# A two-layer network on one core: new places in the instruction order, column groups for two products, keys sent by GpSimd

## The reference, cut to what matters

```python
x = LN(x + attention(x))            # 16 heads of 16 dims, one shared key and value head
x = LN(x + ffn(x))                  # 256 -> 1024, exact GELU, ternary weights, 1024 -> 256
x = LN(x + L1_attn(x))              # see below
x = LN(x + mx_linear(x))            # 256 -> 256, blocks of 32 rounded to an fp6 grid
```

## Time and profile before

| what | value |
|---|---|
| median of 3 runs | 1768.9 us |
| the profiled execution's own time | 1771.4 us |
| its span | 1769.6 us |
| TensorE matmul busy | 1637.5 us (93%) |
| VectorE / ScalarE / GpSimd busy | 1343.4 / 1293.2 / 1104.3 us |
| mean granted TensorE clock | 0.966 of full speed |
| instructions in the span | 84556 |

### The profile page before, as it was taken

How to read it: one execution, slowest core, us unless ns; L and a number is a source line. 1 busy time by engine, 2 the same in 40 slices (tenths; PEclk the granted TensorE clock), 3 DMA queues, 4 the chain that set the end, 5 groups by cost and what they waited for, 6 DMA issues and landing times.

```text
span 1769.6 us, 84556 instructions
## 1 busy us (share of the span) xinstructions
PE 1637.5 (93%) x35371; PEld 1189.0 (67%) x35371; DVE 1343.4 (76%) x2605; ACT 1293.2 (73%) x2601; POOL 1104.3 (62%) x3392
## 2 busy tenths in 40 slices
PE   5768999999999999999999999999999999999865
PEld 4535667677777777677777777777777767776643
DVE  5546778888788888888888888888888888887454
ACT  3437777788787888778887778887788877887521
POOL 5002346767677776676777767777677776767732
PEclk8879999999999999999999999999999999999875
DMA  9963334444244433444333444334443344431010
GB/s 239 203 93 54 60 58 62 74 72 69 51 72 73 73 66 58 67 73 72 70 61 62 74 72 69 61 62 74 71 71 61 62 71 71 73 58 32 18 29 20
DMA packets 133765, 125.18 MB, mean 71 GB/s; under 512 B 18965, under 2 KB 130633, under 8 KB 133385
## 3 DMA queue, kind: packets, MB, share of 16 engines
q1 hardware_dynamic: 129184, 119.50, 39.1%
q10 hardware_dynamic: 4200, 0.27, 0.2%
HBM read 33.73 MB, written 18.87 MB: 30 GB/s over the span
## 4 chain that ended last, share of the span: by engine, by line
PE 53%; POOL 15%; ACT 10%; issue 8%; DVE 4%; DMA 4%; SPq 4%; POOLq 0%; DVEq 0%; ACTq 0%
PE value_bank L772 11%; PE gen_bank L910 8%; PE score_banks L750 7%; PE gen_bank L598 6%; PE max_banks L590 6%; PE gate_bank L803 5%; ACT L1130 4%; ACT probs L1130 3%; PE gen_bank L819 3%; PE gate_bank L598 2%; POOL square L1613 2%; POOL rstd L1598 2%; DMA key_pieces<-khalf 2%; POOL diff L1717 2%; POOL hseq L1722 2%
## 5 line engine op out<-in xcount | busy, mean ns | idle before, releaser
L1186 DVE TENSOR_REDUCE nmax<-max_banks 128x2 f32<-128x1024 f32 x512 | 622.5, 1216 | 65.3 <-PE max_banks L592 61.3
L1130 ACT ACTIVATE probs<-score_banks 128x1024 f32<-128x1024 f32 x512 | 525.0, 1025 | 112.3 <-PE score_banks L752 96.3
L772 PE MATMUL value_bank<-probs,vaug 128*32 128x128 f32 x8192 | 327.3, 278 | 1.1 <-issue 1.1
L772 PEld LDWEIGHTS value_bank<-probs,vaug 128*32 128x32 f32 x8192 | 205.5, 110 | 90.6 <-issue 79.7
L590 PE MATMUL max_banks<-kaug,qaug 62*128 62x512 f32 x512 | 238.7, 466 | 24.8 <-DVE nmax L1186 15.7
L750 PE MATMUL score_banks<-qaug,kaug 64*128 64x512 f32 x512 | 237.6, 464 | 12.4 <-ACT probs L1130 7.8
L1717 POOL TENSOR_TENSOR diff<-gates 128x16 f32<-128x16 f32 x472 | 114.2, 242 | 212.3 <-ACT gates L1135 205.1
L592 PE MATMUL max_banks<-kaug,qaug 62*128 62x512 f32 x512 | 239.2, 467 | 0.4 <-issue 0.4
L752 PE MATMUL score_banks<-qaug,kaug 64*128 64x512 f32 x512 | 237.6, 464 | 0.0
L1135 ACT ACTIVATE gates<-gate_bank 128x48 f32<-128x48 f32 x472 | 99.0, 210 | 167.6 <-PE gate_bank L803 167.2
L803 PEld LDWEIGHTS gate_bank<-hseq,ghT 128*32 128x32 f32 x11328 | 159.1, 112 | 81.3 <-POOL hseq L1722 57.4
(11 more groups left out here) (234 smaller groups left out, 3540.6 us busy)
## 6 DMA issues: line engine op xcount, KB each, us to landing
qstage<-qhalf SPq DMA_DIRECT2D x384, 128.0 KB
qstage<-qhalf SPq DMA_DIRECT2D x128, 112.0 KB
xt<-in_L_attn_x SPq DMA_DIRECT2D x64, 128.0 KB
xk<-in_L_attn_x SPq DMA_DIRECT2D x16, 512.0 KB, 8.7
residual<-x2s SPq DMA_DIRECT2D x64, 128.0 KB
x2f<-residual SPq DMA_DIRECT2D x64, 128.0 KB
out<-x SPq DMA_DIRECT2D x64, 128.0 KB
qaug<-nmT SPq DMA_DIRECT2D x256, 8.0 KB, 1.8
```

The lines of the kernel that those rows point to most:

```text
L772: last = pe.matmul(value_bank[32 * g:32 * g + 32, :].rearrange("p (k t) -> p k t", k=HG)[:, :, u * BLOCK_POS:(u + 1) * BLOCK_POS], vaug[:, ...
L1130: act.activation(probs[:, beat % 2, :, :], score_banks[:, :, :], ACT.Exp).then_inc(exp_done, 1)
L1186: dve.tensor_reduce(nmax[:, m % 2, at:at + 9:8], max_banks[:, :, :], AX_X, ALU.max, negate=True).then_inc(max_taken, 1)
```

## The change

All places are chosen anew. `OWN_AT` gives turns -2 to 5 places of their own, and `place` and `beat_at` look there first; `LAST_AT`, for turn 64, is empty. INPUT stands at -2, which is place 254 of the turn before. HLOA now stands at 260, one turn later. A list `QUARTERED` names what TensorE does in column groups: the same as before, and now also FFN1A, FFN1B and ATT. A transpose in column groups is a matmul with the identity (`turned_block`). `store_keys` and `place_keys` are begun by GpSimd in its set-up instead of by SP.

The diff, cut to its core. Of the eight own turns, three stand here in part; in the others each table is of the same kind.

```diff
-PE_AT = dict(INPUT=0, F2_0=275, F2_1=280, F2_2=285, F2_3=285, F2_4=286, F2_5=288, F2_6=299, F2_7=302, TURND=279, LAST=322, XT=50, Q=12, OUT=128, OT=65, ATT=73, PROJ=90, TURNX=149, B=160, X1T=217, NM=204, FFN1A=247, FFN1B=249)
-ACT_AT = dict(OT=44, TURND=339, XT=104, Q=29, Q8=253, TURNX=196, ATT=145, X1T=230, GELUA=238, GELUB=239, X1=194, X2=178, X4=496)
-DVE_AT = dict(Q=23, X4R=362, X2R=52, OT=62, X3R=171, X3=239, QUANT=240, XN=148, LN1=157, BS=190, SCAN=236, ORDER=182, X1P=216, HLOA=240, NM=216)
-POOL_AT = dict(LN4=418, LN3=97, LN2=6, LNI=8, QIN=192, X2S=77, XD=214, X3B=193, LN1=15, X1B=116, STATES=165, HLOB=219)
-SP_AT = dict(MOVE=15, X2F=200, STORE=89, OUTST=406, XLD=59, NMPLACE=95)
+PE_AT = dict(INPUT=-2, F2_0=274, F2_1=275, F2_2=278, F2_3=278, F2_4=296, F2_5=297, F2_6=299, F2_7=304, TURND=309, LAST=336, XT=63, Q=8, OUT=134, OT=69, ATT=87, PROJ=100, TURNX=173, B=213, X1T=221, NM=217, FFN1A=240, FFN1B=247)
+ACT_AT = dict(OT=43, TURND=307, XT=51, Q=41, Q8=239, TURNX=158, ATT=99, X1T=193, GELUA=224, GELUB=236, X1=151, X2=202, X4=455)
+DVE_AT = dict(Q=27, X4R=371, X2R=85, OT=97, X3R=189, X3=205, QUANT=252, XN=141, LN1=145, BS=215, SCAN=238, ORDER=203, X1P=234, HLOA=260, NM=220)
+POOL_AT = dict(LN4=384, LN3=101, LN2=45, LNI=61, QIN=201, X2S=204, XD=222, X3B=200, LN1=96, X1B=217, STATES=154, HLOB=204)
+SP_AT = dict(MOVE=34, X2F=66, STORE=108, OUTST=365, XLD=46, NMPLACE=71)
 BEAT_AT = dict(
-    SCORES=(19, 61, 89, 107, 137, 157, 178, 231),
-    PAIR=(18, 55, 87, 102, 140, 202, 236, 250),
-    VALUES=(11, 68, 100, 128, 151, 157, 224, 252),
-    STEP=(15, 51, 72, 93, 135, 156, 166, 229),
-    EXP=(86, 121, 165, 181, 186, 227, 228, 236),
-    TANH=(46, 90, 125, 170, 181, 196, 227, 235),
-    MAX=(17, 26, 60, 107, 160, 190, 213, 233),
-    MIX=(3, 4, 12, 13, 20, 34, 96, 157),
+    SCORES=(14, 61, 99, 113, 154, 185, 216, 230),
+    PAIR=(14, 62, 97, 128, 168, 217, 230, 254),
+    VALUES=(3, 87, 111, 130, 180, 203, 227, 240),
+    STEP=(10, 74, 94, 112, 143, 209, 223, 240),
+    EXP=(49, 97, 121, 132, 142, 168, 179, 210),
+    TANH=(34, 66, 101, 128, 137, 174, 198, 224),
+    MAX=(15, 42, 96, 129, 165, 203, 216, 245),
+    MIX=(3, 61, 72, 80, 97, 109, 132, 133),
 )
+OWN_AT = {
...
+    -1: dict(
+        PE=dict(NM=142),
+        DVE=dict(NM=183),
+        SP=dict(NMPLACE=190),
+        BEAT=dict(PAIR=(-1, -1, -1, -1, -1, 36, 197, 211), MAX=(-1, -1, -1, -1, -1, -1, 12, 221)),
+    ),
+    0: dict(
+        PE=dict(XT=1, Q=0, NM=170),
+        ACT=dict(XT=144, Q=28),
+        DVE=dict(Q=11, ORDER=142, NM=142),
+        SP=dict(MOVE=90, XLD=91, NMPLACE=90),
+        BEAT=dict(SCORES=(34, 35, 88, 127, 150, 172, 175, 220), PAIR=(21, 35, 74, 136, 161, 172, 211, 226), VALUES=(-1, 50, 119, 138, 143, 183, 189, 215), EXP=(33, 39, 98, 101, 159, 230, 236, 250), MAX=(10, 14, 89, 102, 133, 141, 209, 243)),
+    ),
...
+    2: dict(
+        PE=dict(F2_0=35, F2_1=35, F2_2=43, F2_3=46, F2_4=47, F2_5=51, F2_6=52, F2_7=56, XT=73, Q=23, OT=81, ATT=94, PROJ=116, TURNX=127, B=151, X1T=182, NM=204, FFN1A=237, FFN1B=240),
+        ACT=dict(OT=10, XT=122, Q=10, TURNX=129, ATT=100, X1T=144, GELUA=187, GELUB=249, X1=133, X2=123),
...
+}
+LAST_AT = dict(
+)
+QUARTERED = ("INPUT", "LAST", "Q", "OUT", "ATT", "PROJ", "B", "FFN1A", "FFN1B")
...
-    def tile_at(table, name, kind, n, at):
-
-        late, slot = divmod(table[name], SLOTS)
+    tables = dict(PE=PE_AT, ACT=ACT_AT, DVE=DVE_AT, POOL=POOL_AT, SP=SP_AT)
+
+    def own(n):
+
+        return LAST_AT if n == TILES else OWN_AT.get(n, {})
+
+    def place(engine, name, n):
+
+        return own(n).get(engine, {}).get(name, tables[engine][name] % SLOTS)
+
+    def tile_at(engine, name, kind, n, at):
+
+        late = tables[engine][name] // SLOTS
         m = n - late + LEAD[kind]
-        return m if at == slot and live(m) and (kind not in ("X", "Q", "LOAD") or n - late >= 0) else None
-
-    def beat_at(name, at):
-
-        return BEAT_AT[name].index(at) if at in BEAT_AT[name] else None
+        return m if at == place(engine, name, n) and live(m) and (kind not in ("X", "Q", "LOAD") or n - late >= 0) else None
+
+    def beat_at(name, n, at):
+
+        slots = own(n).get("BEAT", {}).get(name, BEAT_AT[name])
+        return slots.index(at) if at in slots else None
...
-                slot = PE_AT[name] + SLOTS * (m - LEAD[kind])
+                n = m - LEAD[kind] + PE_AT[name] // SLOTS
+                slot = SLOTS * n + place("PE", name, n)
...
-            def in_quarters(out, weights, moving, start, stop):
-
+            def multiplied(name, out, weights, moving, start, stop):
+
+                if name not in QUARTERED:
+                    return pe.matmul(out(slice(0, P)), weights, moving, start=start, stop=stop, skip_group_check=True)
                 for q in range(0, P, 32):
-                    last = pe.matmul(out(q), weights[:, q:q + 32], moving, start=start, stop=stop, tile_position=(0, q), skip_group_check=True)
+                    last = pe.matmul(out(slice(q, q + 32)), weights[:, q:q + 32], moving, start=start, stop=stop,
+                                     tile_position=(0, q), skip_group_check=True)
                 return last
+
+            def turned_block(name, out, src):
+
+                if name not in QUARTERED:
+                    return pe.transpose(out(slice(0, P)), src, ident[:, :])
+                return multiplied(name, out, src, ident[:, :], True, True)
...
-                    turn_tile(g0, att).then_inc(filled[0], 1)
+                    turn_tile("ATT", g0, att).then_inc(filled[0], 1)
...
-                                    last = pe.matmul(gen_bank[half][:, f * P:(f + 1) * P], w1Tb[:, k, (4 * half + f) * P:(4 * half + f + 1) * P],
-                                                     x1piece[:, piece, k, :], start=(piece + f + k == 0), stop=(piece == 2 and k == KT - 1),
-                                                     skip_group_check=True)
+                                    last = multiplied(("FFN1A", "FFN1B")[half], lambda rows: gen_bank[half][rows, f * P:(f + 1) * P],
+                                                   w1Tb[:, k, (4 * half + f) * P:(4 * half + f + 1) * P], x1piece[:, piece, k, :],
+                                                   piece + f + k == 0, piece == 2 and k == KT - 1)
...
+            def store_keys(r):
+
+                pool.wait_ge(k_split, r + 1)
+                settle(pool)
+                pool.dma_start(k_dram[r].rearrange("t c f -> (t c) f"), khalf[:, :, :].bitcast(F32).rearrange("p a s -> p (a s)")).then_inc(k_written, 16)
+
+            def place_keys(r):
+
+                pool.wait_ge(k_written, 16 * (r + 1))
+                pool.wait_ge(ones_set, 2 * r + 3)
+                settle(pool)
+                for at, g, piece in PLACES:
+                    dims = min(DK, SPLIT - g * DK)
+                    pool.dma_start(kaug[at + g * DK:at + g * DK + dims, r, :, :, :].bitcast(F32).rearrange("d t u s -> d t (u s)"),
+                                 k_dram[r, :, 0:dims, piece * S:(piece + 1) * S].rearrange("t d f -> d t f")).then_inc(k_placed[r], 16)
+
+            for r in range(2):
+                store_keys(r)
+                place_keys(r)
+            store_keys(2)
...
             assert link[0] == BIASES_SPLIT
+            place_keys(2)
+            store_keys(3)
...
+            place_keys(3)
```

More of the change, by code:

```diff
@@ L608, in turn_x @@
                 for k in range(KT):
-                    last = pe.transpose(gen_bank[1][:, k * P:(k + 1) * P], xt[:, m % XR, k * P:(k + 1) * P], ident[:, :])
+                    last = turned_block("XT", lambda rows: gen_bank[1][rows, k * P:(k + 1) * P], xt[:, m % XR, k * P:(k + 1) * P])
                 last.then_inc(filled[1], 1)
@@ L617, in make_queries @@
                     for k in range(KT):
-                        last = in_quarters(lambda q: gen_bank[1][q:q + 32, o * P:(o + 1) * P], wqT[:, k, o * P:(o + 1) * P], xTq[:, k, :],
-                                           k == 0, k == KT - 1)
+                        last = multiplied("Q", lambda rows: gen_bank[1][rows, o * P:(o + 1) * P], wqT[:, k, o * P:(o + 1) * P], xTq[:, k, :],
+                                       k == 0, k == KT - 1)
                 last.then_inc(filled[1], 1)
@@ L781, in input_bias @@
                 wait(pe, tanh_done, STEPS * (m - (bank is not gate_bank)))
-                in_quarters(lambda q: bank[q:q + 32, 0:STEPS * GW], bias_rows, gate_of[:, :, :, :].rearrange("a k g b -> a (k g b)"), True, False)
+                multiplied("INPUT", lambda rows: bank[rows, 0:STEPS * GW], bias_rows[:, :], gate_of[:, :, :, :].rearrange("a k g b -> a (k g b)"), True, False)
             def input_gate(m, bank, g):
                 gate = bank[:, 0:STEPS * GW].rearrange("p (k g b) -> p g k b", k=STEPS, g=3)
-                in_quarters(lambda q: gate[q:q + 32, g, :, :], gcT[:, g, :],
-                            states[:, m // R % 2:m // R % 2 + 1, m % R * STEPS:(m % R + 1) * STEPS, :].rearrange("p a s b -> p (a s) b"),
```

(19 more changed lines are left out.)

97 lines of the change are left out of this document (58 added, 39 removed).

## The result

The changed kernel takes 1906.44 us (median of 4 runs, 1900.80 to 1909.45) beside 1771.12 for the one before on the same chip: a ratio of 1.0761, interval 1.0728 to 1.0794. The forecast was 1812, at most 1865. The direction and the place were right, the size was not: 135 us more instead of 43.

What follows compares the result with a forecast made beforehand. TensorE, busy 93% of the span, was taken as the bound, with the order within a tile and its instruction stream deciding. 1771.4 + 66 - 8 - 16 + 1 = 1814.4 us profiled, less 2.5: 1812 us; range 1745 to 1865.

Steps and rivals of the forecast that it cites:

- The instructions: First layer in column groups: blocks used up before the next comes, stalls 1.8 us a tile, net 1.05, +66 us.
- rival of 1746 us: Instruction fetch keeps up, a block of 1.8 us in the first layer passes without a stop: faster, chance 0.20.
- The order: New places within a tile: +0.5 around the scores, -0.65 later, so -0.15 us a tile, -8 us.
- The queries' wait: Queries' matmul needs the bank the second GELU empties: TensorE waits 0.65 us a tile, which hides stalls.
- The stream: First layer's bf16 column groups take 54 to 56 ns for 128 columns, as whole matmuls do: no gain.
- rival of 109 ns: First layer's groups stream at the f32 group's 109 ns: +160 us, 1972 us, chance 0.01.
- The start: Set-up and first tiles: keys' transfers off SP -3, tile 2's queries sooner -6, own places -7; together -16 us.
- the keys' own waits: Set-up, keys' transfers begun by GpSimd: from a gain of 8 to a loss of 5, taken as -3 us.
- the queries of tile 2: Start: freed from behind the keys in SP's queue, their transfers start 3.5 us sooner: -6 us (-1 to -11).
- +66: Block stalls from column groups, net 1.05 us a tile over 63 tiles, in us; range 0 to +205.
- The end: Last turn makes tile 59's input part for nobody and again for the tail: +1 us (0 to 1.6).
- dearer: Rival: order costs 0.5 to 1 us a tile more, or blocks nearer 4 us: 1840 to 1870, chance 0.20.

Runs made afterwards that it cites:

- small transfers: From tile 9 on, the queries' 8 transfers cut to 4 rows of 1 KB each: 1855 us in the changed kernel, 1769 us with the first layer whole.

## Why the forecast missed, step by step

**The instructions: right in kind, too small.** 359 blocks, stops on borders in runs of 128x32 bf16 matmuls, none when the groups go. I took 3.1 us as the least time between borders; the stops show 3.6. With it the stops in and behind the first layer are 2.10 us a tile, not 1.8: +16 us. (The quickest block that passed without a stop in the kernel before took 4.11 us, not 4.18; nothing hangs on it.) The Trainium skill (Runtime: NRT & Kernel Launch, Instruction fetch mechanics) calls the crossing of such a border "mostly hidden"; here it is for nearly all blocks that last 4 us or more while the DMA engines are idle, and isn't where they last 2.5. Its 2048 instructions for TensorE, which gave my rival of 1746 us, are not borne out: a stretch of 384 dense ones stops already, and no block began less than 1.16 us after the end of its fetch.

**The stops under the queries' transfers: missing.** This step of the forecast failed outright. I had written that the stops of before "fell where the DMA engines had work (share 0.41 between two of them)", and used that only to take the lower figure for the first layer, where the share is 0.08. What the new order puts beside the transfers 5 to 9 us into a tile I didn't count: 0.90 us a tile instead of 0.15, about +40 us.

**The order.** Forecast -0.15 us a tile, measured +0.26 (24.59 without stops against 24.33): +22 us. From the last scores to the next tile's second it gained 0.3 us, not 0.4; the later stretch lost 0.56, not 0.29. A wait that I hadn't found is the turn of the maxima (0.2 to 0.5 us more behind the pair before it). A larger one that the forecast doesn't price is that of the next tile's second scores for the exponentials. TensorE's waits in tiles 9 to 61 of the changed kernel, us in total, times, longest:

```profile
PE score_banks L807 <- ACT probs L1190: 26.1, 53, 0.6
```

The kernel before waited so for 1.4 us in 6 waits, and with x4 behind the GELUs and the first layer whole it is still 28.5 us in 53. How much of the period it costs isn't shown, since no run takes it away. The queries' wait was nearly right, 0.55 in the typical row and 0.45 on the mean for 0.65, and so was its being hidden: the fitted period without stops is 24.07 in the changed kernel and 24.69 with the first layer whole.

**The stream** at 54 ns a bf16 group: right, and the rival of 109 ns is excluded. The Trainium skill (TensorEngine Tiling (Array Packing), Restrictions) has column tiling give up the fast weight load; 2.63 against 2.63 us show no price for it here. fp32 turns, by contrast, went from 0.37 to 0.44, the +0.07 of the forecast.

**The start.** Own places gained 8 to 10 us (7 forecast), but in tiles 0 and 1: the ramp tiles 2 to 8, which were to give the 7, take 160.3 us instead of 161.4 with own places alone. The keys on GpSimd cost 9 to 12 us at tile 9, where the forecast had a gain of 9: 3 for the keys' own waits (a loss of 5 as the worst) and 6 for the queries of tile 2. I had bounded the issues' own time and not what they do to the transfers beside them. SP didn't begin the queries of tile 2 sooner (at 100.45 us, 99.33 before), and they were cast at 120.06 (113.69 before) instead of before 110. Tile 9 starts 8 us later; the forecast had 16 earlier, with some 7 us of its +66 falling into the tiles ahead of tile 9. That is +17 us. **The end** took 3 us less, not 1 more.

1812 + 16 + 40 + 22 + 17 - 4 = 1903, and some 7 for the part of the stops that was not hidden (0.62 us a tile instead of 0.75): 1910 for the 1906 measured. The fitted periods are good to about 0.1 us a tile, 5 us in this sum (the two runs with the first layer whole and the same places give 24.58 and 24.69). The range failed because stops, order and start all missed to the same side: I had given "dearer" one mechanism more, not three.

## What to carry to other kernels

Splitting an operation multiplies TensorE's instructions, and they come in blocks: count, for every point of the loop, how long 256 matmuls and loads last, and keep it above 3.6 us where the DMA engines are idle and near 5.4 us where they are full. These are values of this kernel, not sharp limits: under full engines a stretch of 5.4 us stopped for 0.15 us a tile and one of 4.2 for 0.7 to 0.9, single blocks of 4.0 us passed, and some of up to 7.3 were stopped for. Take the split where it shortens the stream (fp32, 1.05 us a tile) and leave it where it doesn't (bf16). And test an order with the stops taken out: one place on ScalarE was worth some 40 us and could not be seen while TensorE stood at block borders.

## What the runs showed that I had not expected

- Between the start of a fetch and TensorE's going on lie 2.3 to 2.6 us with idle DMA engines and 3.1 to 3.4 with full ones; a fetch takes 0.95 to 1.1 us in the one case and 1.75 in the other, and the fetches of blocks that were stopped for start up to 5.7 us after their border. Single fetches start as late with small transfers too, and what delays those isn't shown.
- 64-column groups cost nothing that can be told (ratio 1.0230 beside 1.0262 whole) where 32-column groups cost 90 us: the price doesn't go by the number of instructions.
- Eight transfers issued by GpSimd took 4.2 to 4.4 us, and SyncE's next eight 8.6 and 8.3 us in two kernels with the keys there, against 5.7 to 6.1 with the keys on SyncE.
